# Attention probabilities scaled on ScalarE before they are transposed, and a prologue made of scheduled steps

## The reference, cut to what matters

```
xn = layernorm(x)                                       # no gain, no bias
# branch 1: causal attention, 16 heads of 64, rotary on q and k
q, k, v = split(xn @ W_qkv);  q, k = rotary(q), rotary(k)
w = softmax(causal(q @ k.T / 8));  a = (w @ v) @ W_out
# branch 2: attention, 16 heads of 8, no mask, then a gated mixture of 8 experts
q, k, v = xn @ Wq + bq, xn @ Wk + bk, xn @ Wv + bv
y  = xn + layernorm(softmax(q @ k.T / sqrt(8)) @ v @ Wo + bo, g1, be1)
f  = y + layernorm(sum over the best 2 experts of prob * (y @ We + bexp), g2, be2)
out = x + a + f
```

## Time and profile before

| | us |
|---|---|
| median of 3 runs (1294.76 to 1302.23) | 1297.58 |
| the profiled execution | 1300.52 |
| its span | 1298.7 |
| PE busy | 1172.0 |
| DVE busy | 939.6 |
| ACT busy | 890.1 |
| POOL busy | 815.1 |
| mean granted clock of TensorE, share of full speed | 0.967 |

### The profile page before, as it was taken

One profiled execution on the slowest core, in us unless ns is written; L12 is line 12 of the kernel. 1 busy time (PEld: TensorE's weight loads), 2 busy tenths in 40 slices (PEclk: granted clock), 3 DMA queues, 4 the chain that ended last, 5 costly groups with the idle time before them and its releaser, 6 DMA issues.

```text
span 1298.7 us, 26053 instructions
## 1 busy us (share of the span) xinstructions
PE 1172.0 (90%) x8393; PEld 757.8 (58%) x8393; DVE 939.6 (72%) x2328; ACT 890.1 (69%) x1840; POOL 815.1 (63%) x733
## 2 busy tenths in 40 slices
PE   4789989999999999989899898989999899999995
PEld 2355656556575665655666465655657456575564
DVE  7657587966878487875879758796587965779555
ACT  3578776686758877568766677657776686667871
POOL 2765784677747784467844678455775566556752
PEclk8899999999999999989999899998999989899998
DMA  4000100011001010010100110001000011001100
GB/s 140 33 34 25 42 25 21 30 50 42 17 33 34 34 41 18 25 34 34 42 17 26 41 42 25 21 22 50 34 30 21 17 42 42 17 25 34 40 11 9
DMA packets 33962, 42.92 MB, mean 33 GB/s; under 512 B 5536, under 2 KB 17060, under 8 KB 33832
## 3 DMA queue, kind: packets, MB, share of 16 engines
q1 hardware_dynamic: 30360, 38.31, 8.5%
q10 hardware_dynamic: 3472, 2.95, 0.7%
HBM read 5.60 MB, written 2.10 MB: 6 GB/s over the span
## 4 chain that ended last, share of the span: by engine, by line
PE 53%; ACT 17%; DVE 16%; issue 11%; POOL 1%; DMA 1%; SPq 0%; ACTq 0%; DVEq 0%; POOLq 0%
PE work L1053 8%; ACT pn L666 7%; PE work L1065 6%; PE work L964 6%; PE work L1118 6%; PE work L1038 5%; ACT fpt L622 5%; PE work L1081 5%; PE work L966 4%; PE work L965 4%; DVE fnmax L816 4%; PE work L1090 4%; PE work L1107 3%; DVE branch L901 2%; DVE work L898 2%
## 5 line engine op out<-in xcount | busy, mean ns | idle before, releaser
L816 DVE TENSOR_REDUCE fnmax<-work 128x2 f32<-128x1024 f32 x256 | 303.4, 1220 | 115.9 <-PE work L1090 114.8
L524 POOL TENSOR_TENSOR raw<-raw,cos_t 128x512 f32<-128x512 f32 x128 | 164.0, 1281 | 292.3 <-DMA swapped<-raw 288.0
L666 ACT ACTIVATE pn<-work,nmax 128x512 f32<-128x512 f32 (+3 forms) x512 | 265.0, 540 | 94.4 <-DVE nmax L916 94.0
L622 ACT ACTIVATE fpt<-work 128x1024 f32<-128x1024 f32 x256 | 251.3, 1033 | 74.5 <-PE work L1107 72.6
L916 DVE CUSTOM_DVE_ANT_0 work<-work,causal 128x512 f32<-128x512 f32 (+3 forms) x512 | 236.1, 521 | 74.5 <-PE work L1038 73.2
L1053 PE MATMUL work<-consts,pn 128*128 128x128 f32 x1280 | 174.0, 282 | 3.0 <-ACT pn L666 1.1
L528 POOL TENSOR_TENSOR raw<-raw,swapped 128x512 f32<-128x512 f32 x128 | 163.4, 1276 | 10.0
L1053 PEld LDWEIGHTS work<-consts,pn 128*128 128x128 f32 x1280 | 146.6, 144 | 36.6 <-DVE fnmax L816 12.5
L539 POOL TENSOR_TENSOR qk_l<-raw,qk_h 128x512 fp32r<-128x512 f32 x128 | 162.8, 1279 | 3.8
L525 POOL TENSOR_TENSOR swapped<-swapped,sin_t 128x512 f32<-128x512 f32 x128 | 163.8, 1279 | 0.0
L675 ACT COPY pt<-work 128x1024 f32<-128x1024 f32 x128 | 128.8, 1014 | 38.3 <-PE work L1053 38.0
(11 more groups left out here) (152 smaller groups left out, 2210.9 us busy)
## 6 DMA issues: line engine op xcount, KB each, us to landing
swapped<-raw SPq DMA_DIRECT2D x256, 128.0 KB, 2.0
x_in<-in_L_attn_x_dram SPq DMA_DIRECT2D x8, 256.0 KB, 3.1
out_dram<-x_in SPq DMA_DIRECT2D x8, 256.0 KB, 2.5
fpt<-in_L_attn_W_qkv_dram ACTq DMA_DIRECT2D x3, 512.0 KB, 6.0
pt<-in_L_ffn_We_dram ACTq DMA_DIRECT2D x1, 512.0 KB, 6.9
wout<-in_L_attn_W_out_dram ACTq DMA_DIRECT2D x1, 512.0 KB, 8.2
pt<-in_rope_dram ACTq DMA_DIRECT2D x1, 192.0 KB, 4.1
affine<-in_L_ffn_g_dram SPq DMA_DIRECT2D x2, 64.0 KB, 4.0
```

The source lines that it names most:

```text
L524: nc.gpsimd.tensor_tensor(raw[:, n % 3], raw[:, n % 3], cos_t[:], ALU.mult)
L622: nc.scalar.activation(fpt[:, ((b * G + g) * T + i) % FP, 2 * r:2 * r + 2].rearrange("p h n -> p (h n)"), bank_of(("fst", b, g, i), 2 * r, 2),
L666: ins = nc.scalar.activation(pn[:, h, PN_AT[j]:PN_AT[j] + n], bank_of(("sc", b, c, unit), h)[:, at:at + n], ACT.Exp, scale=-1.0, bias=nmax ...
L816: nc.vector.tensor_reduce(fnmax[:, j, 2 * r:2 * r + 2, 0:1], bank_of(("fsm", b, g, j), 2 * r, 2).rearrange("p (f n) -> p f n", f=2), AX.X, ...
```

## The change

1. `fan`, `rT`, `rb`, `l_rows` and `l_wide` are gone. A new ACT step `ps`, three per chunk, multiplies `pn` in place by the reciprocals while the queries lie on partitions: 8 activations per chunk, of 512, 384, 256 and 128 columns for each of the 2 heads, with a scale that is a column of `l_inv`. It waits for `inv`, which waits for all `exp` of the chunk. The transposes wait for `ps` of their tile in place of `exp`. `inv` waits for the last `ps` of the chunk before.
2. `div` is now a plain copy out of PSUM, and waits for `pv` alone.
3. `pv` uses four column strips of 32 in place of two of 64: 16 matmuls per chunk in place of 8, each with the same moving columns.
4. The prologue is made of steps (`turn`, `tt`, `tab`, `str`, `strl`, `tb`, `qkb`, `wh`, `wl`, `smh`, `sml`, `bia`, `weh`, `wel`) with places of their own in the lists, and each user in batch 0 waits for what it needs in place of `prepared`. PSUM is cleared by 16 TensorE matmuls with zeros, two on each bank. POOL clears `strips_l` first. ACT loads its table early with one `Exp` of one column, and issues its transfers in another order (the first two thirds of W_qkv ahead of the rotary table). The transfers into `pt` and the causal table have more semaphores of their own.
5. The order tables are new for every step. Batches 0 and 7 have a number of their own for each key (`FIRST`, `LAST`). PSUM banks are assigned anew. On ACT, `ps` stands behind the last `exp` of its chunk, straight behind it in four of the eight chunks and with 1 to 4 other steps between in the others. On DVE, `xn` of the next batch and `nm2` of the batch before, which were neighbours ahead of `inv`, `div` and `fqkl` of the last group, are now five steps apart, with ten more steps between `nm2` and that `fqkl`.

```
-    "fan": [...],   "rT": [...],   "rb": [...],
+    "ps": [-32.586227, -32.076725, -29.333811, ...
+FIRST = { ... one number per step of batch 0 ...
+LAST = { ... one number per step of batch 7 ...
...
+                elif kind == "ps":
+                    c, unit = x_[2:]
+                    act.wait_ge(*after("inv", b, c))
+                    for j, _ in SM_UNITS[unit]:
+                        for h in range(2):
+                            part = pn[:, h, PN_AT[j]:PN_AT[j] + (j + 1) * P]
+                            ins = nc.scalar.activation(part, part, ACT.Copy, scale=l_inv[:, j, h:h + 1])
+                    ins.then_inc(done["ps"], 1)
...
-                            for h in range(2):
-                                pe.wait_ge(*after("exp", b, c, [n for n in range(3) if j in [a for a, _ in SM_UNITS[n]]][0], h))
+                            pe.wait_ge(*after("ps", b, c, [n for n in range(3) if j in [a for a, _ in SM_UNITS[n]]][0]))
...
-                        for h in range(2):
-                            ins = nc.tensor.matmul(psum[h * DH:(h + 1) * DH, i * P:S], v[:, i, 2 * c + h],
+                        for a in range(0, 2 * DH, STRIP):
+                            h = a // DH
+                            ins = nc.tensor.matmul(psum[a:a + STRIP, i * P:S], v[:, i, 2 * c + h, a % DH:a % DH + STRIP],
                                                    pt[:, c % 2, h, PT_AT[i]:PT_AT[i] + S - i * P],
-                                                   start=i == 0, stop=i == T - 1, tile_position=(0, h * DH))
+                                                   start=i == 0, stop=i == T - 1, tile_position=(0, a))
...
-                    dve.wait_ge(*after("rb", b, c))
                     dve.wait_ge(*after("pv", b, c))
-                    nc.vector.tensor_tensor(u[:, c % (NC // 2)], bank_of(("pv", b, c)), l_wide[:], ALU.mult)...
+                    nc.vector.tensor_copy(u[:, c % (NC // 2)], bank_of(("pv", b, c)))...
...
-            nc.vector.memset(work[:], 0.0).then_inc(prep_dve, 1)
+            zeros = strips_l[:].rearrange("p k f c -> p (k f c)")
+            pe.wait_ge(zeroed, 1)
+            for n in range(2 * BANKS):
+                bank = n % BANKS
+                ins = nc.tensor.matmul(work[:, bank * BANK:(bank + 1) * BANK], zeros[:, 0:P], zeros[:, 0:BANK], start=True, stop=True)
...
+            act.wait_ge(cleared, 1)
+            nc.scalar.activation(warm[:], warm[:], ACT.Exp)
...
-                        pe.wait_ge(prepared, 1)
+                        if b == 0:
+                            pe.wait_ge(*after("wl", 0, 2))
```

More of the change, by code:

```diff
@@ L48 @@
 PN_AT = [S + 3 * P, 2 * S, S, 0]
+ONCE = ("turn", "tt", "tab", "str", "strl", "tb", "qkb", "wh", "wl", "smh", "sml", "bia", "weh", "wel")
+LOADED = ("tt", "strl", "tb", "sml", "bia", "wel")
 START = {
[L53 to L68, removed]
@@ new lines @@
+    "ln": {1: 102.443943, 6: 4.519797},
+    "rs0": {1: 74.604155},
+    "xn": {1: 16.208296, 6: -3.017464},
+    "xT": {1: -7.390625, 6: 3.241993},
+    "xh": {1: -3.511749, 6: 1.821731},
+    "xl": {1: -4.076086, 6: -1.683429},
+    "fv": {1: -0.976792, 6: -1.466399},
+    "fvc": {1: 1.278176, 6: -1.16576},
+    "fqk": {1: -1.620944, 6: -0.393475},
+    "fqkh": {1: 0.052844, 6: 0.295247},
+    "fqkl": {1: -1.189394, 6: -1.010939},
+    "fsm": {6: -0.019154},
+    "fmax": {6: -0.019154},
+    "fmT": {1: 0.066856, 6: 0.468386},
@@ new lines @@
+    "nm2": {1: 1.440266, 6: 15.928266},
+    "out": {1: -8.911436, 6: -1.63056},
+    "store": {1: 5.793303, 6: 141.284846},
+    "raw": {1: 0.035501, 6: -0.111242},
+    "swap": {1: 2.323148, 6: 0.004065},
+    "rope": {1: -0.493649, 6: -0.147218},
+    "hi": {1: -0.98275, 6: -0.896027},
+    "lo": {1: -0.778599, 6: -0.20312},
+    "v": {1: 0.070008, 6: -0.066696},
+    "vc": {1: 0.824715, 6: 0.334301},
+    "max": {6: 0.006799},
+    "exp": {6: 0.000836},
+    "tp": {6: -0.035468},
+    "tq": {6: -0.003811},
@@ L237, with later @@
+def later(kind, b, n):
+    own = {0: FIRST, B - 1: LAST}.get(b, {}).get(kind)
+    return own[n] if own else SHIFT.get(kind, {}).get(b, 0)
 ENGINE = {
-    "PE": ("xT", "fv", "fqk", "fsm", "fmT", "fst", "fpv", "fT", "cT", "wo", "x2T", "gate", "moe", "proj", "v", "sc", "tp",
-           "tq", "pv", "rT", "ao"),
-    "ACT": ("xh", "fvc", "fqkh", "fexp", "fo", "ch", "x2h", "gexp", "raw", "vc", "exp", "tpe", "fan", "rb"),
-    "DVE": ("ln", "xn", "xl", "fqkl", "fmax", "fsub", "fdiv", "cl", "ln1", "nm1", "x2l", "gsub", "pick", "moew", "ln2", "nm2",
+    "PE": ("tt", "tb", "xT", "fv", "fqk", "fsm", "fmT", "fst", "fpv", "fT", "cT", "wo", "x2T", "gate", "moe", "proj", "v", "sc", "tp",
+           "tq", "pv", "ao"),
+    "ACT": ("tab", "wh", "smh", "weh", "xh", "fvc", "fqkh", "fexp", "fo", "ch", "x2h", "gexp", "raw", "vc", "exp", "tpe", "ps"),
+    "DVE": ("turn", "str", "strl", "qkb", "wl", "sml", "bia", "wel", "ln", "xn", "xl", "fqkl", "fmax", "fsub", "fdiv", "cl", "ln1", "nm1", "x2l", "gsub", "pick", "moew", "ln2", "nm2",
@@ L249 @@
         KEYS[kind] = [(half,) for half in range(2)]
-    elif kind in ("div", "fan", "inv", "pv", "rT", "rb", "tq", "tqe"):
+    elif kind in ("div", "inv", "pv", "tq", "tqe"):
         KEYS[kind] = [(c,) for c in range(NC)]
@@ L672, in _ @@
                     act.wait_ge(*after("tp", b, c, unit))
+                    if b == 0 and c < 2:
+                        for kind_ in LOADED:
+                            act.wait_ge(*after(kind_, 0))
                     if unit == 0:
```

722 lines of the change are left out of this document (443 added, 279 removed), and 70 rows, old and new, of tables (FIRST, LAST, PSUM, SHIFT).

## The result

The changed kernel takes 1348.25 us (median, 1345.57 to 1349.79) against 1298.18 us for the kernel before on the same chip: ratio 1.0394, 95% interval 1.035 to 1.0438. A second measurement of the same file gave 1347.65 us, ratio 1.0439 (1.0415 to 1.0462). So the changed kernel is 4% slower, by 50 to 56 us, where 9 were forecast and 1333 was the upper end of the range. The profiled execution took 1345.57 us, its span is 1343.6 us; that is 44.9 us more span than before.

A forecast was written before the change was run, and what follows sets the result against it. TensorE, busy 90%, was taken as having least slack, with hand-overs between engines counting too. Batches +29, slow-batch credit -14, `pv` 0, prologue -6 and end 0 made +9 us: 1306.6 us median, range 1268 to 1333.

The forecast's parts named there:

- What bounds: Middle batches: TensorE busy 90% of the span, hand-overs count; four slow batches lose 7 us each at long `xn` and `nm2`.
- TensorE loses `rT`: TensorE, every batch: 256 transposes go, 42.0 us in all, 5.25 us per batch, on the engine with the least slack.
- `ps` at 3.35 us per chunk: ScalarE, every chunk: eight scaling activations added, 3.35 us together; ends 2.0 and 4.1 us.
- +3.8 us per batch: Every batch from the second `xh`: engine overlap stays 3.09 at a time, 155.2 us per batch, +29 us over 7.6 batch lengths.
- -14 us credit for the slow batches: Four slow middle batches: separating `xn` and `nm2` wins back half of their 28 us; bounds 0 and 28.
- `pv` 0: `pv` in four strips: same rate per column, so 0; bounds 6 us gained and 54 us lost.
- Prologue -6: Before batch 0's chunks: first `fsm` near 18 us in place of 24.48, some 6 us gained.
- The end 0, bounds -6 and +6: Last chunk: `ps` joins its chain, but batch 7's separate order may fill as much; taken at 0.
- stretched steps stay: Slow batches: rival in which the long `xn` and `nm2` steps remain, no credit, 1321 us; chance 0.22.
- The fourth: `pv`: rival in which issuing its additional loads and matmuls binds, 54 us more, 1361 us; chance 0.06.
- Cover without gain: Every batch: rival in which scaling fills ScalarE's idle time, freed TensorE time becomes waiting, batch stays 151, 1278 us; chance 0.20.

## Why the prediction was wrong, step by step

- *What bounds*: the reading of the slow batches, two long steps and then a gap, was right. The gap and the 10 us at 0.50 behind it come to 3.9 and 3.3 us, and the long steps are those that meet GpSimd. That hand-overs count was right too.
- *TensorE loses `rT`*: 42 us by the line, called the engine with the least slack. By the page of the kernel without it 32 us of busy time go (1172.0 to 1140.3), and 0.2% of the time. TensorE's slack was never in its busy share.
- *`ps` at 3.35 us per chunk*: right in size. ScalarE's busy time with and without it differs by 221.9 us, 3.47 per chunk; one block of eight takes 3.73 us from end to end. (The lower bound of 2.0 us lay below the 2.3 us that its own slope gave.) The idle time in front of `ps` was forecast at 2 us per batch and is 25.8 us in all, 3.2 per batch. ScalarE came to 1047.5 us against the 1026 in the forecast, TensorE to 1177.6 against 1130.
- *+3.8 us per batch*: this step failed. The overlap of engines, 3.09 at a time, was kept as if it were a constant of the kernel. In the batches that were quick before, it was 9 to 10 us per batch by the first `exp`, 11 by `xh`. With the credit below, the forecast had 29 - 14 = +15 us for the batches; the six in the middle took 22 to 30 more. The runs split it: an order that is slower with no scaling at all (157.9 and 156.7 us where the old order without scaling has 149.8 and 150.1), and on top the scaling's last 63 us.
- *-14 us credit for the slow batches*: failed. The two stretched steps no longer stand before one `fqkl`, as said, and the 4.5 us gaps did go; but in their place every batch got a gap in front of `fst`, the former quick ones too (though filling that gap gained nothing). The four slow batches take 158.2 us in the mean before and 160.1 after. Credit 0.
- *`pv` 0*: right. 2048 records are busy for 152.5 us where 1024 were for 153.1.
- *Prologue -6*: first `fsm` at 20.03 us where 18 was forecast, first `exp` 11.4 us earlier; 9 us of it were gone by the second batch. Kept to the end: nothing measurable, so no run shows the 6 us that the sum has for it. This term and the next were -6 us together; the beginning and the end took 15 to 23 us more.
- *The end 0, bounds -6 and +6*: failed, with the prologue's term. From the first `exp` of batch 7 to the end it is 25.7 us longer. From the first to the last chunk of this batch the old order takes 116.9 us, 11 less than in its quick batches, since the next batch's work is missing; the new order takes 138.5 us, only 4 less than in its batch 3. Without scaling the two are 115.2 and 136.4 us, so it is the order and not `ps`. But much of this is a shift between the marks: from `xh` of batch 7 to the end the new order takes 244.3 us against 250.9, and by that mark the time appears in batch 0 (21.3 us). How it divides between beginning and end is open; no other order of the first or last batch was tried.
- *The rivals*: the nearest was *stretched steps stay*, on the slow side (no credit, 1321 us), with a TensorE gap in every batch and a low clock behind it. Such a gap came at another step and through another wait: 1.87 to 3.6 us for `nm1` in front of `fst`, with 6.8 us at 0.50 behind it. The steps themselves did not stay as they were: between 560 and 1060 us `xn` takes 1.40 us and `nm2` 3.1 in each of four batches, where both took 4.4 to 4.5 before. That its number comes nearest is luck. The fourth is refuted by `pv`'s busy time. "Cover without gain" described what `rT` is worth, but not that it would hold for the whole.

The sum as it should have been, from these runs: order 1.9% (25 us), the scaling on top 2.2 to 2.6% (29 to 34 us), old normalisation removed -0.2%, strips 0. That is 51 to 56 us of the 50 to 57 measured. Why the order costs 25 us is open. TensorE is at half clock for 158 us in it against 65 us in the old order without scaling, and busy 40 us longer (1180.0 and 1140.3), but filling the gap halved the half clock in the middle batches and the medians lie 3 us apart. What is shown is where the time lies: 12 us in the middle batches, which have lost the quick kind, and 20 at the beginning and the end.

## What to carry to other kernels

An engine's work can be free up to a point and dear beyond it: here 159 us more on ScalarE cost nothing, the next 63 us cost 30, and TensorE's waits say that it is for the steps queued behind the block; so price added work by who is queued behind it, and measure it with half and with a token of it. Leaving a suspected cost out altogether (a kernel without its normalisation) is the cheapest way to learn what removing it can bring at most; here that was 0.2%, a tenth of what the scaling cost. Where TensorE bounds and stands a few microseconds per round, matmuls of no use in that gap are worth trying before any reordering (in the old order four gaps of 4.5 us filled gave 0.5 to 1.0%, in the new one filling gained nothing), placed ahead of the wait and into a bank that the awaited step does not free.

## What the runs showed of the hardware that was not expected

- With 18 matmuls of 512 columns (4.39 us) in a 4.5 us gap the granted clock was 1.00 behind it, where it was 0.50 for 10 us; four such gaps filled are worth 0.5 to 1.0% of the kernel. Eight of them in the changed kernel's gaps of 1.87 to 3.6 us also closed the gaps, but the 6.8 us at 0.50 were gone in only three of the seven batches; in three 3.4 us stayed, and in the last there were 10.2.
- Behind gaps of 1.87 to 3.6 us in front of `fst` stood 6.8 us at half clock, in all seven batches of the changed kernel. There it cost nothing that can be measured: with the gap filled, a batch at full clock throughout took 158.6 us, and the other middle batches of the two kernels 157.4 to 164.2.
- An in-place scaling on ScalarE of a single column takes 286 ns as recorded (and adds 185 ns of busy time), 128 columns 390, 512 columns 717.
- VectorE's `tensor_scalar` between SBUF operands, with the second head scaled there: 279 ns for 128 columns and 487 for 512 while no GpSimd instruction ran, 278 to 1624 ns when one did. With GpSimd busy 56% of the span, the means are 533 and 724 ns, so that 128 columns cost three quarters of 512.
